# Attention kernel of four chained layers: softmax shift and denominators moved to the query-major layout, per group of four heads

## The reference, cut to what matters

```python
q = ((seq2 + b_self) @ Wq + bq)          # seq2 is the side input f, seq1 is x
k = concat(seq1 + b_prev, seq2 + b_self) @ Wk + bk
v = concat(seq1, seq2) @ Wv + bv
score_prev = einsum('bhqd,bhkd->bhqk', q, k[:, :, :512]) * SCALE   # masked beyond seq_len1
score_self = (q * k[:, :, 512:]).sum(-1) * SCALE                   # one per query and head
weights = softmax(concat(score_prev, score_self))                  # over 513 entries
attn = weights[..., :-1] @ v[:, :, :512] + weights[..., -1:] * v[:, :, 512:]
x = x + attn @ Wo + bo
```

## Time and profile before

| | |
|---|---|
| time, median of 3 runs | 1429.83 us (1429.33 to 1430.75) |
| profiled execution: span, first to last instruction | 1427.7 us |
| instructions | 22882 |
| PE busy | 1320.6 us (92%) |
| DVE busy | 930.6 us (65%) |
| ACT busy | 880.7 us (62%) |
| POOL busy | 430.4 us (30%) |
| mean granted TensorE clock | 0.975 of full speed |

### The profile page before, as it was taken

How to read it: one execution, slowest core, us unless ns; L and a number is a source line. 1 busy time by engine, 2 the same in 40 slices (tenths; PEclk the granted TensorE clock), 3 DMA queues, 4 the chain that set the end, 5 groups by cost and what they waited for, 6 DMA issues and landing times.

```text
span 1427.7 us, 22882 instructions
## 1 busy us (share of the span) xinstructions
PE 1320.6 (92%) x7009; PEld 560.8 (39%) x7009; DVE 930.6 (65%) x1594; ACT 880.7 (62%) x1853; POOL 430.4 (30%) x372
## 2 busy tenths in 40 slices
PE   4799999899998999889998899989999999999995
PEld 1332354324633255332553235432354324533253
DVE  6386458864688546975569654896458864688444
ACT  2398536974378834877448764587536874378731
POOL 5331026310443105331064201651026310443114
PEclk8899999999999999999999999999999999999996
DMA  4213012130120302212021301213012130120200
GB/s 159 70 45 99 1 36 69 38 107 1 53 71 28 99 15 59 62 65 52 31 56 49 115 1 31 74 38 108 1 41 65 45 100 1 54 73 24 69 1 30
DMA packets 62204, 76.26 MB, mean 53 GB/s; under 512 B 14378, under 2 KB 35174, under 8 KB 62062
## 3 DMA queue, kind: packets, MB, share of 16 engines
q1 hardware_dynamic: 62062, 74.54, 18.4%
HBM read 40.81 MB, written 8.40 MB: 34 GB/s over the span
## 4 chain that ended last, share of the span: by engine, by line
PE 61%; ACT 13%; DVE 12%; issue 11%; DMA 1%; POOL 1%; DVEq 0%; ACTq 0%; SPq 0%; POOLq 0%
PE bank L441 22%; PE banks L441 12%; DVE nmx L974 7%; PE bank L1319 7%; PE banks L1303 6%; ACT banks L734 6%; PE bank L1164 5%; ACT big L786 5%; PE banks L1237 3%; PE bank L1266 2%; PE bank L1329 1%; PE bank L1271 1%; PE bank L1293 1%; DVE y L1020 1%; PE bank L1224 1%
## 5 line engine op out<-in xcount | busy, mean ns | idle before, releaser
L734 ACT ACTIVATE banks<-banks,nmx 128x512 f32<-128x512 f32 x512 | 340.5, 671 | 55.8 <-DVE nmx L974 53.1
L974 DVE TENSOR_REDUCE nmx<-banks 128x1 f32<-128x512 f32 x512 | 325.9, 683 | 69.7 <-PE banks L1237 67.9
L786 ACT ACTIVATE big<-banks 128x1024 f32<-128x1024 f32 x256 | 247.9, 1021 | 64.5 <-PE banks L1303 49.7
L441 PE MATMUL bank<-fT,w_hi 128*128 128x512 f16 x768 | 244.0, 379 | 0.8
L1237 PE MATMUL banks<-KQ 97*128 97x512 f16 x512 | 154.1, 382 | 39.5 <-ACT banks L734 36.9
L516 POOL TENSOR_TENSOR big<-x,b2r 128x512 f32<-128x512 f32 x32 | 40.6, 1268 | 438.6 <-DVE x L909 397.5
L1303 PE MATMUL banks<-KQ 98*128 98x512 f16 x512 | 146.7, 396 | 23.5 <-ACT big L786 18.6
L441 PE MATMUL bank<-fT,w_lo 128*128 128x512 f16 x384 | 145.5, 379 | 0.0
L1319 PE MATMUL bank<-big,V 128*32 128x512 f32 x1024 | 142.2, 629 | 0.0
L477 POOL TENSOR_TENSOR half<-qk,ones 128x512 f16<-128x512 f32 x64 | 66.6, 1040 | 240.0 <-ACT qk L716 240.0
L441 PEld LDWEIGHTS bank<-fT,w_hi 128*128 128x128 f16 x768 | 74.7, 97 | 90.9 <-issue 11.9
(11 more groups left out here) (142 smaller groups left out, 1987.6 us busy)
## 6 DMA issues: line engine op xcount, KB each, us to landing
KQ<-half SPq DMA_DIRECT2D x384, 64.0 KB, 2.0
tiles_in<-in_x_dram SPq DMA_DIRECT2D x32, 256.0 KB, 7.1
tiles_in<-in_fside_BxSxS_dram SPq DMA_DIRECT2D x32, 256.0 KB, 2.7
x<-in_x_dram SPq DMA_DIRECT2D x8, 1024.0 KB, 5.4
out_dram<-x SPq DMA_DIRECT2D x32, 256.0 KB, 2.1
w<-in_L_cond_W_dram SPq DMA_DIRECT2D x16, 256.0 KB, 4.6
b2r<-in_L_cond_b_dram SPq DMA_DIRECT2D x8, 256.0 KB, 4.5
gr<-in_L_cond_gamma_dram SPq DMA_DIRECT2D x8, 256.0 KB, 5.3
```

The lines of the kernel that those rows point to most:

```text
L441: mm = eng.matmul(out_ap, pairs[n][0], pairs[n][1], start=(first and n == 0), stop=(last and n == len(pairs) - 1))
L734: ins = eng.activation(bank(step, i)[:, j % 2, :], bank(step, i)[:, j % 2, :], ACT.Exp, bias=nmx[:, t, h:h + 1], accum_out=esum[:, t, h:h ...
L786: eng.activation(big[:, n % 2, 2 * u:2 * u + 2, :], bank(step)[:, :, :], ACT.Exp).then_inc(read(step), 1)
L974: eng.tensor_reduce(nmx[:, t, h:h + 1], bank(step, i)[:, j % 2, :], AX_X, ALU.max, negate=True).then_inc(max_done, 1)
```

## The change

- The shift is made for each group g as soon as its last maximum is there (new step SHIFT, after the eighth SMAX of a group), with queries on the partitions: a minimum on 128x16, a DVE transpose in blocks of 32x32 into `shiftT`, and four transfers of 16 rows of 64 bytes each into the shift row of `KQ`. The first score matmul of a group waits for that group's transfers.
- SELF writes each group into a bank use of its own; ACT copies it out negated on 128x128 (for each group, in place of NEG), a new step SELFT transposes it on PE, and DVE copies 128x16 of it.
- One DVE instruction reads both tiles of an SMAX step and writes two maxima. ACT waits once, for this instruction, and then computes both exponentials.
- DEN (in place of MROW) takes the two differences on 128x64 and ACT their exponentials on 128x128. SROW first forms denominators, reciprocals and self weights on 128x64 on DVE; then PE transposes them (four transposes of 32 columns), and DVE splits the transposed rows.
- `KQ` is laid out as [group, key or query, head, position] in place of [head, group, key or query, position]. The mask row is filled with four transfers in place of one. `head_rows` has eight rows of selectors in place of four (sixteen affine selects).
- The load of the next x waits for the last read of SROW in place of `norms_done`.

```diff
@@ order_mid
         if maxima and i >= opens[maxima[0][1]]:
             out.append(maxima.pop(0))
+            if not maxima or maxima[0][1] != out[-1][1]:
+                out.append(("SHIFT", out[-1][1]))
         elif not maxima and not rows:
-            out.append(("MROW",))
+            out.append(("DEN",))
...
-        if step == ("VS", 2):
-            later.setdefault(i + PARTS - 1, []).append(("NEG",))
+            later.setdefault(i + 2 * PARTS + 3, []).append(("SELFT", step[1]))
@@ gpsimd
             for n, low in enumerate((0, LOW_ROW)):
-                for g in range(NG):
+                for r in range(2 * NG):
...
-                    eng.affine_select(out=v, in_=v, compare_op=ALU.not_equal, fill=1.0 / RS, base=-g - low,
-                                      pattern=[[-NG, NJ], [0, DH]], channel_multiplier=1).then_inc(sel_ready, 1)
+                    eng.affine_select(out=v, in_=v, compare_op=ALU.not_equal, fill=1.0 / RS, base=-r * NJ - low,
+                                      pattern=[[-1, NJ], [0, DH]], channel_multiplier=1).then_inc(sel_ready, 1)
@@ sync
-                            eng.dma_start(KQ[MASK_ROW:MASK_ROW + 1, :, :, 0, :].rearrange("o j g n -> o (j g) n"),
-                                          row.to_broadcast([H, S]).rearrange("(o h) n -> o h n", o=1)
-                                          ).then_inc(mask_in, 16)
+                            for m in range(NG):
+                                eng.dma_start(KQ[MASK_ROW:MASK_ROW + 1, m, 0, :, :],
+                                              row.to_broadcast([NJ, S]).rearrange("(o h) n -> o h n", o=1)
+                                              ).then_inc(mask_in, 16)
...
-                    elif step[0] == "MROW":
-                        wait_read(eng, step, b)
-                        eng.dma_start(KQ[SHIFT_ROW:SHIFT_ROW + 1, :, :, 1, :].rearrange("o j g n -> o (j g) n"),
-                                      shift[:, :]).then_inc(shift_in, 16)
+                    elif step[0] == "SHIFT":
+                        g = step[1]
+                        eng.wait_ge(shift_flip, b * NG + g + 1)
+                        rows = KQ[SHIFT_ROW:SHIFT_ROW + 1, g, 1, :, :].rearrange("o j (t m n) -> o (j t) m n", t=NT, n=32)
+                        for m in range(P // 32):
+                            eng.dma_start(rows[:, :, m, :], shiftT[32 * m:32 * m + TJ, g, :]).then_inc(shift_in[g], 16)
@@ scalar
                         t, q = divmod(u, 2)
+                        eng.wait_ge(max_done, b * MAXIMA + g * 2 * NT + u + 1)
                         for j in (2 * q, 2 * q + 1):
-                            eng.wait_ge(max_done, b * MAXIMA + (g * 2 * NT + u) * 2 + j % 2 + 1)
-                            h = NG * j + g
+                            h = j * NT + t
...
-                    elif kind == "NEG":
...
-                            op = eng.activation(self2[:, 0, t * P:(t + 1) * P], lone[3][t * DH:t * DH + H, 0:P],
-                                                ACT.Copy, scale=-1.0)
-                        op.then_inc(read(("SELF", 0)), NG)
-                    elif kind == "SROW":
+                    elif kind == "SELF":
+                        g = step[1]
+                        wait_full(eng, step, b)
...
+                        eng.activation(self_rows[:, g % 2, :], bank(step, i)[:, 0:P], ACT.Copy, scale=-1.0
+                                       ).then_inc(read(step, i), 1)
+                    elif kind == "DEN":
                         eng.wait_ge(self_diff, b * 2 + 2)
-                        eng.activation(self2[:, :, :], self2[:, :, :], ACT.Exp).then_inc(self_exp, 1)
+                        eng.activation(ediff[:, :, :, :], ediff[:, :, :, :], ACT.Exp).then_inc(self_exp, 1)
@@ vector
-                        for j in (2 * q, 2 * q + 1):
-                            h = NG * j + g
-                            eng.tensor_reduce(nmx[:, t, h:h + 1], bank(step, i)[:, j % 2, :], AX_X, ALU.max,
-                                              negate=True).then_inc(max_done, 1)
+                        eng.tensor_reduce(nmx[:, g, :].rearrange("p (j t) -> p j t", j=NJ)[:, 2 * q:2 * q + 2, t],
+                                          bank(step, i)[:, :, :], AX_X, ALU.max, negate=True).then_inc(max_done, 1)
+                    elif kind == "SELFT":
...
+                        eng.tensor_copy(nself[:, g, :].rearrange("p (j t) -> p j t", j=NJ),
+                                        bank(step, i)[:, 0:P].rearrange("p (t n) -> p n t", t=NT)[:, 0:NJ, :]
+                                        ).then_inc(read(step, i), 1)
+                    elif kind == "SHIFT":
+                        g = step[1]
+                        eng.wait_ge(max_done, b * MAXIMA + (g + 1) * 2 * NT)
+                        wait_read(eng, ("SELFT", g), b)
+                        eng.tensor_tensor(shift16[:, g, 0:TJ], nmx[:, g, :], nself[:, g, :], ALU.min
+                                          ).then_inc(shift_min, 1)
+                        eng.wait_ge(shift_min, b * NG + g + 1)
...
+                        eng.transpose(shiftT[:, g, :], shift16[:, g, :]).then_inc(shift_flip, 1)
+                    elif kind == "DEN":
+                        eng.wait_ge(shift_min, b * NG + NG)
+                        eng.tensor_tensor(ediff[:, 0, :, :], shift16[:, :, 0:TJ], nmx[:, :, :], ALU.subtract
+                                          ).then_inc(self_diff, 1)
+                        eng.tensor_tensor(ediff[:, 1, :, :], shift16[:, :, 0:TJ], nself[:, :, :], ALU.subtract
+                                          ).then_inc(self_diff, 1)
                     elif kind == "SROW":
...
+                        eng.tensor_tensor(dens[:, :, :], esum[:, :, :], ediff[:, 0, :, :], ALU.mult).then_inc(den, 1)
+                        eng.wait_ge(den, b * 3 + 1)
+                        eng.tensor_tensor(dens[:, :, :], dens[:, :, :], ediff[:, 1, :, :], ALU.add).then_inc(den, 1)
+                        eng.wait_ge(den, b * 3 + 2)
+                        eng.reciprocal(nrm[:, :, :, 0, :], by_tile(dens[:, :, :])).then_inc(den, 1)
+                        eng.wait_ge(den, b * 3 + 3)
+                        eng.tensor_tensor(nrm[:, :, :, 1, :], nrm[:, :, :, 0, :], by_tile(ediff[:, 1, :, :]), ALU.mult
+                                          ).then_inc(norms_done, 1)
                         wait_full(eng, step, b)
+                        eng.tensor_scalar(norms16[0:NR, :], bank(step, i)[0:NR, :], RS, None, ALU.mult
+                                          ).then_inc(norms_hi, 1)
...
+                        eng.scalar_tensor_tensor(out=norms16[LOW_ROW:NROWS, :], in0=bank(step, i)[0:NR, :], scalar=RS,
+                                                 in1=norms16[0:NR, :], op0=ALU.mult, op1=ALU.subtract
+                                                 ).then_inc(read(step, i), 1)
@@ tensor
                     elif kind == "SROW":
-                        wait_read(eng, ("SMAX", NG - 1, 2 * NT - 2), b)
-                        wait_read(eng, ("SMAX", NG - 1, 2 * NT - 1), b)
+                        eng.wait_ge(norms_done, b + 1)
                         wait_free(eng, step, b)
@@ tensor, scores
+                if k == 0:
+                    eng.wait_ge(shift_in[g], i * DMAS_PER_SHIFT + DMAS_PER_SHIFT)
@@ tensor, attention
-                eng.wait_ge(shift_in, i * 16 + 16)
```

More of the change, by code:

```diff
@@ L165, in plan_banks @@
             m += 1
-        elif step[0] in ("MROW", "SROW"):
-            give({"MROW": 4, "SROW": 6}[step[0]], step)
-    for g in range(NG):
-        give(3, ("SELF", g))
+        elif step[0] in ("SELF", "SELFT"):
+            give(3, step)
+        elif step[0] == "SROW":
+            give(2, step)
     for g in range(NG):
@@ L386, in build_program @@
         mask_in = sem("mask_in")
-        shift_in = sem("shift_in")
+        shift_in = [sem(f"shift_in{g}") for g in range(NG)]
         max_done = sem("max_done")
-        MAXIMA = H * NT
-        self_neg = sem("self_neg")
+        MAXIMA = 2 * NT * NG
+        shift_min = sem("shift_min")
+        shift_flip = sem("shift_flip")
         self_diff = sem("self_diff")
@@ L611, in params @@
                 rlang = eng.value_load(idx[0:1, bass.ds(i + 2 * B, 1)], min_val=0, max_val=RLANGS - 1)
-                eng.wait_ge(norms_done, i + 1)
+                wait_read(eng, ("SROW",), i)
                 eng.dma_start(x1[:, :, :], whole(x, i)).then_inc(x_in, 16)
@@ L856, in _ @@
             for j in range(NJ):
[L857 to L859 removed]
+                eng.memset(head_cols[DH * j:DH * j + DH, j:j + 1], 1.0 / WS).then_inc(rows_ready, 1)
             eng.wait_ge(full[2], 1)
@@ L1215, in mid @@
                         if g == 0 and not tail:
-                            eng.wait_ge(rows_ready, 4 + H)
-                        if g == 0:
-                            wait_free(eng, step, b)
+                            eng.wait_ge(rows_ready, 4 + NJ)
+                        wait_free(eng, step, b)
```

(32 more changed lines are left out.)

104 lines of the change are left out of this document (44 added, 60 removed).

## The result

The changed kernel takes 1476.03 us (median; 1474.42 to 1476.42) against 1429.58 us (1429.27 to 1430.75) for the kernel before on the same chip: a ratio of 1.032, 95% interval 1.0307 to 1.0333. That is 46.5 us slower, where 30.7 were forecast. The profiled span grew from 1427.7 to 1472.4 us, by 44.7.

A forecast was written before the change was run, and what follows sets the result against it. Bound: a loop of waits between PE, DVE and ACT. Loop elements 21.4, first element 4.3, end 1.6, constants 3.4 sum to 30.7 us on 1427.7, plus 2.1: 1460.5 us; own range 1448 to 1474, whole range 1437 to 1484.

The forecast's parts named there:

- The joined maximum: SMAX steps: one DVE instruction for two tiles takes 1.21 us; ACT's first exponential, where it waits, starts 0.53 us later.
- 2.12 + 0.53 + 0.32 - 0.6: Per loop element: four late handovers 2.12 us, PE's wait at 402.46 0.53, longer bank-pair round 0.32, DVE's shorter instructions -0.6.
- nine handovers: First batch element: the chain passes from DVE straight to ACT nine times, each 0.53 us later, 4.8 us together.
- Self scores, SELFT and SHIFT: Loop element: net 0.79 us less without NEG's copies, 0.27 more for an ACT copy, 1.2 more for small DVE instructions.
- The end of the stretch: From last fill to V's last block: PE stalls 0.7 us before SROW's transposes; 0.2 us more per element, 1.6 in all.
- The early load of x: Load of the next x, issued earlier at the end of the stretch: taken to be off the path.
- Constants: Setup: eight more affine selects put the KQ fills and the weight split back by 3.4 us, split starting at 24.
- the variant given one in five: Setup: DVE's cast comes before POOL's fill, mask operation waits only for the first fill, some 6 us lower; one in five.
- slack hides the handover: Maxima stretch: PE's other work absorbs the later handover; only first element, end and constants remain: +8, 1438 us; chance 0.17.
- DVE's queue decides: Maxima stretch: filled pairs always wait for DVE, each step saves 0.06 us; 21 us less, 1408 us; chance 0.13.
- The round that binds everywhere: Maxima stretch: 16 of 32 steps each cost 0.53 us unabsorbed, 8.3 us per loop element, 1499 us; chance 0.12.

## Why the prediction was right or wrong

**The joined maximum: right, in kind and size.** Priced at 1.21 us, measured 1.222. The first exponential 1.24 us after DVE's start, measured 1.26. The terms that belong to it (2.12 + 0.53 + 0.32 - 0.6) give 2.37 us for a loop element; taking it out of the changed kernel gave 2.26. In the first element nine handovers were priced at 4.8 us; 5.6 measured. The two halves of the sum come out near as well: the handover costs 3.10 (terms 2.97), the shorter instruction with its 0.06 us earlier handover returns 0.84 (term 0.6). The close fit is partly luck. The handovers were counted on the chain of the kernel before, and there the same join cost 1.66 us and not 2.37; in the changed kernel, whose other steps had also moved, they were never counted.

**Self scores, SELFT and SHIFT: right.** The remaining terms (0.27 for the copy in ACT's run, -0.79 for NEG, +1.2 for DVE) give 0.68 us; the stretch with two maxima is 57.05 against 56.57, 0.48 more. The transpose no row had shown took 0.212 us, the ACT copy 0.279, both near the low end, as chosen.

**The end of the stretch: half right.** The stall of PE in front of SROW's transposes was forecast at 0.7 us and is 0.66; the reciprocal on 64 elements at 0.56 and is 0.55. V's last copy is 0.39 us later in the six passages with a jump, with 0.2 forecast; in the first passage it is 1.12 us earlier (4.70 us after the last fill, 5.82 before), which the prediction did not treat apart.

**The early load of x: wrong, and this is the step that failed.** The prediction put it as "The early load of x is off the path as well." It asked when x is needed and not what the transfer meets on its way. The load's start moved from behind `norms_done`, where ACT already runs attention, to 0.95 us ahead of the end of V's last copy, and its first packets so in front of the code packet that ACT's start follows. The gap of 2.24 us was in the rows and read as fixed. Moving the load away gave 14.0 us, and giving it to the kernel before brought part of the gap there (3.25 to 3.74 us in place of 2.2, 6.3 us in all). With it the sum of 30.7 comes to 44.7 (30.7 + 14.0), the measured growth of the span; that the two agree so closely is chance, since the other terms miss by up to 2 us on both sides and the 14.0 is a difference of medians (12.6 by the spans).

**The two do not add up from separate runs.** Join alone 13.6 us, early load alone 6.3, all together 46.5. The late handover delays V's copy by 0.46 us, and that takes the lead of the load from 0.43 us (gap 2.2) to 0.95 (gap 4.2). In the changed kernel the join costs 38.6 us: 16.1 + 5.6 in the stretches, 0.46 x 6 = 2.8 behind them, 11.7 in six gaps, and 2.4 that I did not place.

**Constants: right in place, short by 1.1 us.** The weight split starts at 24.89 us (24 forecast, 20.68 before), the first fill is 4.5 us later (3.4 forecast). The 1.1 us are no more than this setup varies: with the same setup the first fill was at 70.12 us at a granted clock of 0.83, and at 71.43 at 0.78 in the kernel with two maxima.

```profile
2.70 6.97 POOL L472 TENSOR_SCALAR_AFFINE_SELECT p_both<-p_both 64x128 f32<-64x128 f32 x16
...
10.36 6.92 POOL L479 MEMSET KQ<- 32x8192 f16 x1
...
10.41 7.42 DVE L878 CAST head_rows<-p_both 64x1024 f16<-64x1024 f32 x1 [3.04 <-POOL t L475]
...
17.33 7.36 POOL L481 MEMSET KQ<- 32x8192 f16 x1
17.75 7.22 DVE L879 TENSOR_SCALAR half<-t,lens_f 8x512 f16<-8x512 f32 x1
24.89 2.27 DVE L883 SCALAR_TENSOR_TENSOR w_lo<-big,w_hi 128x2048 f16<-128x2048 f32 x1
```

The cast did not get ahead of the fill, the variant given one in five. Both fills still cover a DVE operation each.

**The rivals.** That slack hides the handover (1438) and that DVE's queue decides (1408) are out by the stretch of 59.31 us and by the waits. The round that binds everywhere (1499) asked for 8.3 us more in a loop element; 2.77 came. The time of 1476 lies inside the range of 1437 to 1484, but 2 us above the forecast's own range of 1448 to 1474. It is inside because the upper part had been left for that rival; the cause that filled it was another one, and that is luck.

## What to carry to other kernels

Where a producer hands tiles to a consumer over few buffers and waits are on the chain, the first result of a joined instruction counts, and not its total. The handovers on the chain times the delay give the size, no more: here 2.37 us for an element, where 1.66 and 2.26 were measured in two kernels. A transfer that is issued earlier can cost though nobody needs it and nobody waits for it: look at what else the DMA engines must deliver there, above all at a loop's jump back, where ACT stood on "issue" here until 1.7 to 2.0 us after a code packet. A gap that the chain calls "issue" beside a transfer is worth one run with the transfer moved by a microsecond, and an operation of microseconds where its size asks for tenths is worth one with its neighbour moved away.

## What was not expected of the hardware

- The gap of ACT at the jump follows a code packet of 8 KB. With the load's lead over the end of V's copy at 0.43 us the gap was 2.1 to 2.3 us, at 0.84 it was 3.25 to 3.74, at 0.95 it was 3.8 to 4.6, and with the load after the copy 2.0 to 2.5. That q14 carries ACT's code is read from this order in time; no row names the engine a code packet is for.
- PE passes the same jump with 1.07 us of "issue" in the changed kernel, where ACT has 4.07: the engines are held up unequally.
- A fill of 32x8192 on POOL took 6.92 us beside the weight split and 7.36 beside the mask operation, which is 8x512 and took 7.22 us there in place of 0.47. The cast of 64x1024 in the changed kernel took 7.42 us beside a fill and 0.69 with the fill held back.
- Why the join costs 1.66 us in the kernel before and 2.26 in the changed one was not tried apart. Nor was a load of x without the tables behind it.
